# Gathering the first expert tile on TensorE, and holding the second expert's weights behind the row stores, in a one-core perceiver block

## The reference

```python
x = x + cross_attention(layernorm(x), ctx)
x = x + self_attention(layernorm(x))            # 16 heads, rotary positions
xf = layernorm(x).reshape(T, D)                 # T = 1024, D = 512
scores = sigmoid(xf @ gate_w.T + balance_bias)  # 8 experts
top, idx = top_k(scores, 2)
top = top / (top.sum(-1) + 1e-6)
h = silu(einsum('td,ehd->teh', xf, w1))         # 1024 hidden features
expert_out = einsum('teh,edh->ted', h, w2)
x = x + einsum('te,ted->td', comb(top, idx), expert_out)
```

## Time and profile before

| | before |
|---|---|
| median of 3 runs | 568.65 us (567.06 to 568.94) |
| profiled execution, its own time | 566.58 us |
| its span | 564.5 us |
| granted TensorE clock, mean | 0.938 |
| PE / DVE / ACT / POOL busy | 86% / 67% / 45% / 20% |
| end of the row stores | 296.3 us into the span |
| start of the first expert product | 303.7 us |
| start of the second tile's product | 315.3 us |

### The profile page before, as it was taken

How to read it: one execution, slowest core, us unless ns; L and a number is a source line. 1 busy time by engine, 2 the same in 40 slices (tenths; PEclk the granted TensorE clock), 3 DMA queues, 4 the chain that set the end, 5 groups by cost and what they waited for, 6 DMA issues and landing times.

```text
span 564.5 us, 11023 instructions
## 1 busy us (share of the span) xinstructions
PE 485.6 (86%) x3598; PEld 276.2 (49%) x3599; DVE 380.8 (67%) x850; ACT 252.9 (45%) x392; POOL 111.0 (20%) x88
## 2 busy tenths in 40 slices
PE   5979989998898999767505799999999999999992
PEld 2734536645574868453402345444544445444441
DVE  5768897578979898887883666763665637663230
ACT  1404545644478494837201456551634426542130
POOL 1022212114050404003830011121112111121112
PEclk9999899999999999977556799999999999999998
DMA  8997669800049991441785477886674856743222
GB/s 312 402 395 291 224 237 404 333 1 0 1 159 380 380 364 44 150 150 75 262 266 149 129 234 235 231 271 168 201 221 105 264 140 205 223 80 70 56 56 38
DMA packets 56128, 111.56 MB, mean 198 GB/s; under 512 B 25216, under 2 KB 26272, under 8 KB 50976
## 3 DMA queue, kind: packets, MB, share of 16 engines
q1 hardware_dynamic: 25152, 87.64, 43.0%
q10 hardware_dynamic: 26640, 13.73, 10.2%
q0 software_dynamic: 4304, 9.77, 8.1%
HBM read 76.19 MB, written 29.43 MB: 187 GB/s over the span
## 4 chain that ended last, share of the span: by engine, by line
PE 59%; DVE 20%; DMA 6%; issue 5%; POOL 5%; ACT 2%; SPq 2%; ACTq 0%; POOLq 0%; DVEq 0%
PE bank L718 20%; PE bank L736 19%; PE bank L539 5%; PE bank L355 4%; DMA ctx_region<-in_ctx 4%; PE bank L523 3%; POOL routed_rows L1675 3%; DVE small L1083 2%; DVE small L1080 2%; DVE ctx_region L1326 1%; DMA routed_rows<-shared,ints 1%; PE bank L616 1%; POOL small L1610 1%; DVE ctx_region L1328 1%; PE bank L504 1%
## 5 line engine op out<-in xcount | busy, mean ns | idle before, releaser
L718 PE MATMUL bank<-wbuf,ctx_region 128*128 x504 | 115.9, 388 | 6.3 <-issue 5.1
L1460 DVE SCALAR_TENSOR_TENSOR wbuf<-ctx_region,wbuf 128x2048 f32 (+1 forms) x28 | 62.9, 2289 | 32.5 <-ACT wbuf L902 32.5
L1705 POOL DMA_INDIRECT out<-misc,ints x21 | 38.6, 1839 | 229.8 <-ACT misc L983 175.0
L718 PEld LDWEIGHTS bank<-wbuf,ctx_region 128*128 128x128 f16 x504 | 48.8, 100 | 65.6 <-issue 13.1
L902 ACT ACTIVATE wbuf<-ctx_region 128x2048 f32 (+1 forms) x28 | 51.9, 1902 | 29.5 <-issue 29.5
L736 PE MATMUL bank<-wbuf,actT 128*128 x264 | 58.8, 379 | 1.0 <-DVE actT L1570 1.0
L1610 POOL TENSOR_TENSOR small<-small 128x2 f32<-128x2 f32 (+2 forms) x25 | 27.0, 1086 | 163.5 <-DVE small L1056 160.8
L1002 ACT ACTIVATE ctxT_region<-bank 128x512 f32<-128x512 f32 x42 | 25.1, 597 | 67.2 <-PE bank L718 67.2
L736 PE MATMUL bank<-wbuf,xn 128*128 x240 | 53.4, 379 | 0.0
L539 PE MATMUL bank<-ctx_region,wbuf 128*128 128x256 f16 x384 | 43.3, 273 | 3.7 <-DVE ctx_region L1211 3.7
L1564 DVE CAST ctxT_region<-ctxT_region 128x1024 f16<-128x1024 f32 x21 | 14.6, 694 | 42.1 <-ACT ctxT_region L1002 42.1
(11 more groups left out here) (220 smaller groups left out, 777.5 us busy)
## 6 DMA issues: line engine op xcount, KB each, us to landing
ctx_region<-in_experts SPq DMA_DIRECT2D x28, 1024.0 KB
routed_rows<-ctxT_region SPq DMA_DIRECT2D x1, 16900.0 KB, 50.7
ctxT_region<-in_ctxT SPq DMA_DIRECT2D x8, 1542.0 KB, 12.6
ctx_region<-in_ctx SPq DMA_DIRECT2D x8, 1536.0 KB, 9.2
ctx_region<-routed_rows ACTq DMA_DIRECT2D x23, 260.0 KB, 4.1
wbuf<-in_experts SPq DMA_DIRECT2D x4, 1024.0 KB
out<-x ACTq DMA_DIRECT2D x8, 256.0 KB
wbuf<-in_wqT SPq DMA_DIRECT2D x4, 256.0 KB, 5.4
```

Source lines behind the costliest of these rows:

```text
L718: mm = nc.tensor.matmul(bank[half][:, :], xgT[:, b, x_part, k * P:(k + 1) * P], w16[:, ds(at + (w_part + k * EH + half * 512), 512)], star ...
L1460: nc.vector.scalar_tensor_tensor(w16[:, ds(at + (LOW + n * PIECE), PIECE)], src_[:, piece], W_SCALE, w16[:, ds(at + (HIGH + n * PIECE), PI ...
L1705: nc.gpsimd.indirect_dma_start(out, bass.IndirectOffsetOnAxis(idx[:, slot_no:slot_no + 1].bitcast(U32), axis=0), y_out[:, slot_no, :], Non ...
```

## The change

**The first expert's first tile.** It is no longer read back from DRAM. DVE writes for each token tile a block `hot` of 128 x 128 zeros and ones: a one at (token, r) if this token is row r of the first expert's region. PE multiplies the token tile's f16 rows by it and sums over the eight tiles, which gives the 128 rows already transposed in two PSUM banks (high and low part). ACT copies the two banks out as `xgT`. The first product is ordered anew: all passes with the high weights first, then the low weights, each step waiting for the piece that it needs.

**Other moves.** The low part of the last pair's features is cut by DVE and not by POOL. `choose` is split in two; the ranking of tiles 4 and 5 runs between the residual adds of tiles 6 and 7. DVE cuts all four low pieces of the first expert's weights before it looks at the loaded rows. ACT loads silu's table ahead of the copies, and loads rows 0 and 1 after them. SP holds the second expert's weights until all 16 row stores have landed.

The diff, shortened where lines only rename or drop what is replaced:

```diff
+CHOSEN = 4096.0
             sp.wait_ge(s["z_ps"], TILES)
+            sp.wait_ge(s["scattered"], 16 * 2 * TILES)
             for e in range(1, E):
                 load_expert(e, stage)
...
+            def first_rows(tiles):
+                for tile in tiles:
+                    pe.wait_ge(s["hot"], tile + 1)
+                    pe.wait_ge(s["xf_lo"], tile + 1)
+                    for part in range(2):
+                        for k in range(KC):
+                            at = part * D + k * P
+                            mm = nc.tensor.matmul(bank[4 + part][:, k * P:(k + 1) * P], xf16[:, tile, at:at + P], hot[:, tile, :],
+                                                  start=False, stop=(tile == TILES - 1), skip_group_check=True)
+                if tile == TILES - 1:
+                    mm.then_inc(s["xgT_ps"], 1)
+            pe.wait_ge(s["x_post"], TILES)
+            pe.wait_ge(s["zrow"], 1)
+            for part in range(2):
+                nc.tensor.matmul(bank[4 + part][:, :], nothing[:, 0:P], nothing, start=True, stop=False, skip_group_check=True)
+            first_rows(range(0, ROUTED[0][1]))
             pe.wait_ge(s["rt_slots"], 2)
             choices_before(2)
-            pe.wait_ge(s["rt_map"], 1)
-            def first_rows_T():
-                pe.wait_ge(xg_in[0], 16)
-                transposes(bank[4][:, :].bitcast(F16), [xg16[:, 0, k * P:(k + 1) * P] for k in range(2 * KC)],
-                           s["xgT_ps"], ident16)
+            first_rows(range(ROUTED[0][1], TILES))
+            def first_tile_product():
+                pe.wait_ge(s["xgT0"], 1)
+                for w_part, x_parts in ((HIGH, (0, 1)), (LOW, (0,))):
+                    for half in range(2):
+                        for k in range(KC):
+                            if w_part == LOW:
+                                pe.wait_ge(s["w1_lo"], k // 2 + 1)
+                            else:
+                                pe.wait_ge(s["w_hi"], k // 2 + 1)
+                            for x_part in x_parts:
+                                mm = nc.tensor.matmul(bank[half][:, :], xgT[:, 0, x_part, k * P:(k + 1) * P], ...)
+                        if w_part == LOW:
+                            mm.then_inc(s["h_ps"], 1)
-            first_rows_T()
-            first_product(0, 0, experts_of(0)[0], first=True)
+            first_tile_product()
+            pe.wait_ge(s["rt_map"], 1)
             hidden_T(0)
...
             cut_high(expert0, 2 * EXPERT, (3,), 0)
+            nc.scalar.activation(sc_nb, neg_half[:, 0:2], ACT.Silu)
+            act.wait_ge(s["xgT_ps"], 1)
+            for part in range(2):
+                op = nc.scalar.copy(xgT[:, 0, part, :], bank[4 + part][:, :])
+            op.then_inc(s["xgT0"], 1)
             act.wait_ge(s["rt_map"], 1)
             act.wait_ge(s["scattered"], 16 * 2 * TILES)
             load_rows(0, 0)
             load_rows(1, 1)
-            hidden(0, 0, 16, first=True)
+            silu(0)
+            rows_T(1, 16)
+            act.wait_ge(s["fields"], 2)
+            load_rows(2, 0)
             hidden_copy(0, 0)
...
+                    if pair + 1 == PAIRS and t == 0:
+                        choose_rank(1)
...
+            def last_features_low():
+                for t in range(2):
+                    tile = TILES - 2 + t
+                    dve.wait_ge(s["xf_hi"], tile + 1)
+                    nc.vector.tensor_tensor(xf16[:, tile, D:2 * D], ln4_n[:, t, :], xf16[:, tile, 0:D], ALU.subtract)\
+                        .then_inc(s["xf_lo"], 1)
...
+                dve.wait_ge(s["rt_sel"], n + 1)
+                then(nc.vector.scalar_tensor_tensor(hot_at[:, some], sel[:, some, 0], -CHOSEN, slot[:, some, 0], ALU.mult, ALU.add))
+                for tile in range(lo, hi):
+                    ts(hot[:, tile, :], const("places"), hot_at[:, tile:tile + 1], None, ALU.is_equal).then_inc(s["hot"], 1)
...
-            choose(1)
+            choose_gates(1)
             place(1)
+            last_features_low()
             logits_out(PAIRS - 1)
-            choose(2)
+            choose_rank(2)
+            choose_gates(2)
             place(2)
...
-            cut_low(expert0, 2 * EXPERT, (0, 1), 0)
-            first_rows_copy()
+            cut_low(expert0, 2 * EXPERT, (0, 1, 2, 3), 0)
             rows_fields(0, 0, 16, again=False)
-            cut_low(expert0, 2 * EXPERT, (2, 3), 0)
+            cut_hidden(0)
             rows_fields(1, 1, 16, again=False)
-            cut_hidden(0)
...
             scatter(0, 1, ROUTED[0][1])
-            features_low(PAIRS - 1)
             scatter(1, *ROUTED[1])
             scatter(2, *ROUTED[2])
```

45 lines of the change are left out of this document (25 added, 20 removed).

## The result

| | before | after |
|---|---|---|
| median on one chip, 6 runs each | 567.86 us (564.36 to 568.94) | 554.15 us (553.27 to 555.97) |
| profiled execution, its own time | 566.58 us | 555.97 us |
| its span | 564.5 us | 554.1 us |
| granted TensorE clock, mean | 0.938 | 0.955 |

The ratio is 0.9757, 95% interval 0.9729 to 0.9786: 13.8 us faster. I had forecast 558.3, in a range from 555.0 to 562.0, so the median lies 0.85 us under the range. The profiled execution was forecast at 556.3 and took 555.97, and tile 1's product starts at 305.10 where I had 305.0. That agreement is luck: two differences of 2 us cancel in it.

A forecast was written before the change was run, and what follows sets the result against it. DVE's queue sets tile 1's product, 10.7 us earlier less 0.4 for the crossed transpose: 10.3 us. Profiled execution 566.58 less 10.3 is 556.3; median 568.65 - 10.3 = 558.3 us, range 555.0 to 562.0.

The forecast's parts named there:

- What bounds the kernel: Start of tile 1's product: DVE's queue sets it, 10.7 us earlier; from there each microsecond is one off the end.
- the late norm: Routing: ranking between residual adds pushes tile 7's add by about 0.95 us, so last logits end about 276.5.
- nearly nothing is gained up to here: DVE's routing up to the row numbers: ready at 282.9, against 283.8 before.
- The stall: DVE's first compare of the last group, 2.68 us beside POOL's low parts, falls to 0.29: 2.39 us back.
- The last low parts: Last pair's features, two operations of 128x512 moved from POOL to DVE: 1.3 to 1.4 us together.
- the added 3.5 us use up the stall and the gaps: DVE ahead of the row numbers: added operations cost 3.5 us, so nearly nothing is gained there.
- The 0.4 us that I added for the transpose: Tile 1's transpose: weight pieces cross it, so tile 1 starts at 305.0 and not 304.6.
- Rival 2: Routing earlier: clock at 2.4 GHz in denser PE work, 0.6 plus 2.5 us more, 555 us; chance 0.12.
- The rows: Row stores land at 290.5, 3.0 us after issue; rows 0 at 296.0, rows 1 about 297: not late.
- rival 1: Crossing weights hold rows or transpose longer: tile 1 starts at 308, gain 7, 561.5 us; chance 0.2.
- The second expert's weights: Loads start at about 290.9, 15 us later; pieces are there 2 to 4 us before use: free.
- Clock: Tile 1's product: between a gain of 2.5 us and a loss of 2.7, no change taken.

The follow-up runs named there:

- the fourth piece moved: Changed kernel with the fourth low weight piece cut behind the hidden values and not ahead: 557.44 us, ratio 0.98.
- the third one: Third profile, from the third timing of the unchanged changed kernel, on another chip: 556.56 us, ratio 0.9789.
- the piece was held: Wide gather, split map, rows 1 loaded first, one more tile stored early, plus second expert's second piece held until tile 1's transpose landed: 556.43 us, ratio 0.9793.
- count first: Changed kernel with the last group's count ahead of all 64 gather matmuls, not behind 32 of them: 555.37 us, ratio 0.9784.
- wide gather with the split map: Changed kernel with 512-column gather matmuls plus transposes, and two low pieces cut in mid-map, two behind the hidden values: 556.5 us, ratio 0.9807.
- wide gather: Changed kernel with the gather in 16 matmuls of 512 columns and 8 transposes, not 64 of 128 columns: 556.01 us, ratio 0.9785.
- the second profile: Profile from the second timing of the unchanged changed kernel, on another chip: 558.83 us, ratio 0.9855.
- the map split: Changed kernel with row loads released early, two low pieces cut in mid-map and the last two behind the hidden values: 556.05 us, ratio 0.9784.

## Why the prediction was right or wrong

**What bounds the kernel: right.** The loop carries what is won ahead of it one for one, and DVE's queue set its start; the first is shown by the last column of the table, the second by the fourth piece moved.

**The size: 1.9 us too little.** On the ruler the forecast was a gain of 62.4 - 52.1 = 10.3 us, and the profile shows 12.2, the third one 12.3. The step that failed is the late norm: "They wait for the norm, so they now end about 276.5", 0.95 us later than before, from which I had that "nearly nothing is gained up to here". The terms, against the profile that the forecast was made from:
- PE's last logits end 0.05 us later and not 0.95. The add of tile 7 is 0.6 us later, near the forecast, but the delay did not carry on. From the start of the last features' transposes to that of the logits it is 3.01 us before and 2.44 after. Between them PE counts tiles 4 and 5. Before, it waited there for their ranking until 271.16; after, the ranking had been moved ahead, and the count starts at 273.34, while the transposes run to 273.55. I had followed the ranking's cost to the norm, and not what waited for it. First two rows of before, then two of after:

```profile
269.00 1.94 PE L355 MATMUL bank<-consts,misc 128*128 128x128 f32 x8 [3.49 <-DVE misc L1059]
271.16 1.00 PE L587 MATMUL bank<-ctxT_region,consts 128*128 128x16 f32 x4 [0.23 <-DVE ctxT_region L1420]
```

```profile
271.61 1.94 PE L359 MATMUL bank<-consts,misc 128*128 128x128 f32 x8 [5.21 <-DVE misc L1098]
273.34 0.87 PE L591 MATMUL bank<-ctxT_region,consts 128*128 128x16 f32 x4
```

- The stall came back as forecast, 2.4 us: the last group's first compare starts 23.0 us behind the ruler's compare in both kernels, and the gates are ready at 27.3 against 29.7. From that compare to the row numbers it is 6.0 us, where the forecast had 6.1 (276.8 to 282.9).
- The last low parts, 1.29 us, lie for the most part in the wait for the logits (0.81 us of it can be seen in before, 1.78 in the kernel with the low parts on POOL). The forecast's numbers go from the logits on and don't charge them; only its words do, "the added 3.5 us use up the stall and the gaps".
- Together the row numbers came 1.9 us earlier, where I had 0.9: 1.0 us of the miss.
- The other 0.9 are small ones. The map with its blocks took 7.85 us and not 8.0; the four pieces and the fields, to the cast right behind them, 8.85 and not 9.35: 0.65 us together. The 0.4 us that I added for the transpose cost 0.2.

How the miss divides rests on one profile of before. Against the second, with its earlier clock, the row numbers are only 0.6 us earlier and the logits 1.4 us later, and the loop still 11.8 us earlier. So 1.5 to 1.9 us too little at the loop is firm, and the share of the routing in it is not.

**Rival 2 gave 555 us, near the measured 554.15, but its mechanism did not come.** It wanted the clock at its full level for the gather and the loop. The granted clock was 0.50 from 268.52 to 282.18, the first 32 gather matmuls took 3.62 us, and tile 1's product 7.50.

**The rows: right.** The last store landed within 2.8 us of its issue; neither loads nor transpose were late. Crossing weights did not slow the changed kernel's transpose: SP issued pieces at 296.10 and 300.89, and the transpose between them (299.05) took 3.15 us, as long as where the piece was held. At other distances behind a piece it took 4.08 us (count first), 4.50 (wide gather with the split map), 6.14 (wide gather) and 7.42. Beside these stands the Trainium skill, "DMA: Bandwidth & Descriptors", section on queues, rings and completion order, which I had weighed in the forecast. The slow ones agree with it. The 3.15 us in the changed kernel show that the price it led me to, that of rival 1, isn't always paid.

**The stall of DVE beside POOL: right.** 2.68 us fell to 0.29, and came back at 2.67 with the low parts on POOL. In all four profiles with the low parts on POOL beside that compare (2.68, 2.72, 1.95 and 2.67 us) it ends 0.15 to 0.17 us after POOL's second operation. By the Trainium skill, "GPSIMD Engine Reference", section on specifications, POOL shares its SBUF interfaces with VectorE, in contention with DVE instructions that have two SBUF inputs. The trace agrees, and shows it in the other direction too (2.79 against 0.96 us for a store).

**The second expert's weights: free, as forecast,** in the changed kernel: ACT cuts them at 303.00 without a wait.

**Clock: right in sum.** Tile 1's product takes 7.50 us, against 7.65 before; 7.08 in the second profile.

**The median.** The forecast took one execution's sum over to the median, 2.0 us above it as in the kernel before; in the first timing the median lies 1.8 us below the profiled execution. The changed kernel's medians in three timings are 554.15, 558.83 and 556.56 us, and 558.3 lies among them. The ratios give 13.8, 8.2 and 12.0 us. The loops explain 11.8 to 12.3 without the slow stretch and 8.7 to 9.0 with it. That the 558.83 comes from runs that mostly had the stretch is argued, from its one profile; the third timing, 12.0 us with a profile free of it, fits that theory in neither of the two bands that were expected for its median (554 to 555, or 557 to 559). And some 1.6 us of the first timing's 13.8 stay unexplained by the profiled pair, with the interval's near end at 12.2.

## What to carry to other kernels

Work that is put on the engine that sets the end is free as far as it lies in a wait that this engine has anyway; look for that wait before charging it. When a step is moved earlier, ask who waited for it at its old place. Count from a mark just ahead of the change, not from the start of the span, or a scatter of up to 4 us will hide or feign a result of that size, and take a second profile of the kernel before as well, since the mark itself left 1.4 us open here. After an early start is won, the next transfer in line decides: with the map split the cast moved by 4.8 us and the loop by 2.3.

## What the runs showed of the hardware

- A run of 128-column f16 matmuls can fall from about 0.07 us to 0.71 us for one, for 2 to 6 us in all, shortly after the granted clock has risen; in four of the five cases DVE then waited 3.6 us for a count whose matmuls were through. 512-column matmuls in its place didn't show it, in four profiles in which PE paused within 1.0 us of the rise. The cause is open.
- A DVE compare of 128x128 with both inputs in SBUF, 0.29 us alone, took 1.95 to 2.72 us beside POOL's two subtractions, and ended with the second of them.
- POOL's indirect store takes 0.96 us in most places, and took 2.79 beside DVE's cut of the low weights, an operation with two inputs in SBUF.
- A transpose by DMA took 3.15 us with no weight piece in its way, and 3.15 to 7.42 us where it crossed pieces of 1 MB, 7.42 when it was issued 1.3 us behind a piece.
